# Expert stages: the gated half of the up products as three float32r products, and scatters without clears between them

## The reference

```python
h_NM2H = jnp.einsum('md,ndh->nmh', x_MD, Wl1) + bl1[:, None, :]
a_NMH, b_NMH = (h_NM2H[..., :H], h_NM2H[..., H:])
y_NMD = jnp.einsum('nmh,nhd->nmd', jax.nn.silu(a_NMH) * b_NMH, Wl2) + bl2[:, None, :]
ew_MN = ew_MN.at[jnp.arange(M)[:, None], idx_MK].set(val_MK)
y_MD = jnp.einsum('mn,nmd->md', ew_MN, y_NMD)
```

## Time and profile before

| | before |
|---|---|
| time, median of 3 runs | 1177.89 us (1176.38 to 1179.65) |
| the profiled execution, its own time | 1185.97 us |
| its span, first to last instruction | 1184.1 us |
| mean granted TensorE clock | 0.834 |
| PE busy | 842.3 us (71%) |
| POOL busy | 731.5 us (62%) |
| DVE busy | 705.8 us (60%) |
| ACT busy | 571.2 us (48%) |
| DMA moved | 142.69 MB, 121 GB/s |

### The profile page before, as it was taken

The page is one execution under the profiler, slowest core; times in us unless marked ns, Lnnn a source line. Parts: engine busy times, 40 slices in busy tenths (PEclk is TensorE's granted clock), DMA queues, the critical chain, the costliest instruction groups (busy, mean ns, idle before and its releaser), DMA issues.

```text
span 1184.1 us, 19270 instructions
## 1 busy us (share of the span) xinstructions
PE 842.3 (71%) x4480; PEld 667.6 (56%) x4481; DVE 705.8 (60%) x2510; ACT 571.2 (48%) x1588; POOL 731.5 (62%) x1127
## 2 busy tenths in 40 slices
PE   3787867767429889898755667566721988988981
PEld 1565656646318778787722334333420877877871
DVE  5697867845524444444647888889750343655555
ACT  3776646642213233333768887988620333323320
POOL 3017876736745777777710378787784576766774
PEclk9779878866659999999977888778755999999996
DMA  6022232112255555556412232231233555777874
GB/s 182 19 59 86 89 87 76 53 36 70 79 129 166 148 155 155 157 155 196 129 54 71 85 98 80 76 95 45 60 104 79 153 153 179 230 216 227 241 211 138
DMA packets 160255, 142.69 MB, mean 121 GB/s; under 512 B 17817, under 2 KB 133154, under 8 KB 160070
## 3 DMA queue, kind: packets, MB, share of 16 engines
q1 hardware_dynamic: 121744, 70.98, 21.9%
q10 hardware_dynamic: 20854, 37.24, 10.3%
q0 software_dynamic: 17600, 33.87, 8.4%
HBM read 93.47 MB, written 50.37 MB: 121 GB/s over the span
## 4 chain that ended last, share of the span: by engine, by line
PE 43%; ACT 17%; DVE 11%; issue 11%; POOL 7%; another core or an unknown queue 6%; DMA 2%; ACTq 2%; DVEq 1%; SPq 0%; POOLq 0%
PE banks L1055 16%; PE banks L1075 6%; POOL queue_dram L567 5%; PE banks L927 4%; PE banks L953 4%; ACT qkv L737 2%; ACT hmix L636 2%; PE banks L960 2%; PE banks L1110 2%; ACT gated L746 2%; PE banks L1063 2%; PE banks L1111 2%; PE banks L981 1%; DVE gated L1403 1%
## 5 line engine op out<-in xcount | busy, mean ns | idle before, releaser
L580 POOL DMA_INDIRECT result_dram<-ytile,result_row x284 | 277.9, 979 | 165.4 <-remote 57.5
L567 POOL DMA_INDIRECT queue_dram<-hffn,place_i x256 | 300.3, 1173 | 60.4 <-issue 46.0
L1055 PE MATMUL banks<-xt,tile_up 128*128 128x256 f32 x1136 | 286.2, 397 | 35.8 <-DVE gated L1403 31.6
L746 ACT ACTIVATE gated<-banks,tile_bias 128x256 f32<-128x256 f32 x284 | 119.2, 473 | 302.7 <-PE banks L1055 130.5
L1055 PEld LDWEIGHTS banks<-xt,tile_up 128*128 128x128 f32 x1136 | 213.4, 198 | 69.2 <-issue 28.3
L1403 DVE SCALAR_TENSOR_TENSOR gated<-banks,tile_bias,gated 128x256 f32<-128x256 f32 x284 | 124.2, 480 | 170.9 <-ACT gated L746 104.5
L1075 PE MATMUL banks<-wdown_sb,gated 128*128 x1136 | 156.4, 281 | 17.4 <-DVE ytile L1411 9.1
L1075 PEld LDWEIGHTS banks<-wdown_sb,gated 128*128 128x128 f32 x1136 | 142.0, 195 | 22.1 <-issue 21.7
L542 POOL MEMSET spacer<- 128x176 f32 x508 | 133.2, 262 | 0.4
L557 POOL COPY hffn<-top_f 128x4 f32<-128x4 f32 x32 | 5.0, 190 | 203.6 <-DVE place_i L1301 203.6
L1411 DVE TENSOR_TENSOR ytile<-banks,down_bias_sb 128x256 f32<-128x256 f32 x142 | 59.5, 419 | 76.1 <-remote 41.4
(11 more groups left out here) (203 smaller groups left out, 1570.2 us busy)
## 6 DMA issues: line engine op xcount, KB each, us to landing
tile_up<-w_up ACTq DMA_DIRECT2D x142, 256.0 KB
xtile<-queue_dram SPq DMA_DIRECT2D x142, 130.0 KB
qkv<-result_dram SPq DMA_DIRECT2D x24, 512.0 KB
x_dram<-xres SPq DMA_DIRECT2D x32, 256.0 KB
result_dram<-ytile,result_row POOLq DMA_INDIRECT x284
xin<-x SPq DMA_DIRECT2D x16, 256.0 KB
xold<-x SPq DMA_DIRECT2D x16, 256.0 KB
queue_dram<-hffn,place_i POOLq DMA_INDIRECT x256
```

What stands on the lines that cost most here:

```text
L567: nc.gpsimd.indirect_dma_start(queue_dram, bass.IndirectOffsetOnAxis(ap=place_i[s][:, at:at + 1], axis=0), hffn[s][c][:, j, :], None).then ...
L580: nc.gpsimd.indirect_dma_start(result_dram, bass.IndirectOffsetOnAxis(ap=result_row[i % SLOTS][:, h:h + 1], axis=0), ytile[i % SLOTS][:, h ...
L746: last = nc.scalar.activation(gated[i % GSLOTS][:, h, :], ps_up[i % 2][:, h, :], ACT.Silu, bias=tile_bias[i % STEP][:, h:h + 1])
L1055: last = nc.tensor.matmul(ps_up[i % 2][:, h, :], tile_up[i % WSLOTS][:, h * P:(h + 1) * P], xt[i % 2][:], start=True, stop=True)
```

## The change

On PE, `up` keeps the two float32 matmuls of the silu half, on `xt`. Each of the two matmuls of the gated half becomes three float32r matmuls into the same accumulator: head of the weights by head of x, head of the weights by rest of x, rest of the weights by head of x. The heads are the values as a float32r write rounds them, the rests are what is left; the product of the two rests is left out.

- The weights are split once, on GpSimd, before its first scatter: three DMAs of 1 MB each in a chain through an SBUF buffer, a copy and a subtraction of [128, 2048], and two DMAs of 1 MB out. The expert stages then load 384 KB a tile from `up_dram` and not 256 KB from the input.
- x is split a tile: `empty_x` on ACT gets a second copy ahead of the old one, and DVE gets `rest_of_x(i+4)`, a subtraction of 128x256 behind `add_bias(i)`. PE waits for it (`rest_ready`) before the first float32r matmul.
- In the expert stages the scatters have no clear between them. In the scatters of routed rows the clears stay; one semaphore wait (`numbered`) goes.
- Three startup semaphores become one.

```diff
@@ POOL
-                    last = nc.gpsimd.tensor_copy(hffn[s][c][:, :, D], k_sb[:, bass.ds(at + (K_TOKEN + c * TPC), TPC)])
-                last.then_inc(numbered, 1)
+                    nc.gpsimd.tensor_copy(hffn[s][c][:, :, D], k_sb[:, bass.ds(at + (K_TOKEN + c * TPC), TPC)])
...
-                pool.wait_ge(numbered, m)
-                pool.sem_inc(place_taken, 1)
...
                             ytile[i % SLOTS][:, h, :], None, bounds_check=NO_RESULT - 1, oob_is_err=False).then_inc(y_stored[i % SLOTS], 16)
-                        space(i * XPARTS + h, count * XPARTS)
...
+            ups = w_up.rearrange("p (e a n) -> p e a n", a=2, n=HID)
+            head, rest = up_parts
+            plain = rest[:].bitcast(F32)
+            pool.dma_start(plain, ups[:, :, 0, :]).then_inc(up_moved, 16)
+            pool.wait_ge(up_moved, 16)
+            pool.dma_start(up_dram[:, :, 0, :], plain).then_inc(up_moved, 16)
+            pool.wait_ge(up_moved, 2 * 16)
+            pool.dma_start(plain, ups[:, :, 1, :]).then_inc(up_moved, 16)
+            pool.wait_ge(up_moved, 3 * 16)
+            nc.gpsimd.tensor_copy(head[:], plain).then_inc(up_split, 1)
+            pool.wait_ge(up_split, 1)
+            nc.gpsimd.tensor_tensor(rest[:], plain, head[:].bitcast(F32), ALU.subtract).then_inc(up_split, 1)
+            pool.wait_ge(up_split, 2)
+            for i, part in enumerate(up_parts):
+                pool.dma_start(up_dram[:, :, 1 + i, :], part[:].bitcast(F32)).then_inc(up_moved, 16)
@@ ACT
                     act.wait_ge(xtile_turned, done(f, t))
+                    nc.scalar.activation(x_parts[i % 2][:, 0, :], ps_xt[i % 2], ACT.Copy)
                     nc.scalar.activation(xt[i % 2][:], ps_xt[i % 2], ACT.Copy).then_inc(xt_ready, 1)
...
-                    nc.scalar.dma_start(tile_up[i % WSLOTS][:], w_up[:, bass.ds(e * (2 * HID), 2 * HID)]).then_inc(tile_up_in[i % WSLOTS], 16)
+                    nc.scalar.dma_start(tile_up[i % WSLOTS][:], up_dram[:, bass.ds(e, 1), :, :].rearrange("p e k n -> p (e k) n")).then_inc(tile_up_in[i % WSLOTS], 16)
...
+                act.wait_ge(up_moved, 5 * 16)
@@ PE
-                    for h in range(2 * HCH):
-                        last = nc.tensor.matmul(ps_up[i % 2][:, h, :], tile_up[i % WSLOTS][:, h * P:(h + 1) * P], xt[i % 2][:],
-                                                start=True, stop=True)
+                    for h in range(HCH):
+                        nc.tensor.matmul(ps_up[i % 2][:, h, :], tile_up[i % WSLOTS][:, 0, h * P:(h + 1) * P], xt[i % 2][:],
+                                         start=True, stop=True)
+                    pe.wait_ge(rest_ready, done(f, t))
+                    for h in range(HCH):
+                        head, rest = (tile_up[i % WSLOTS][:, 1 + part, h * P:(h + 1) * P].bitcast(F32R) for part in range(2))
+                        dst = ps_up[i % 2][:, HCH + h, :]
+                        nc.tensor.matmul(dst, head, x_parts[i % 2][:, 0, :], start=True, stop=False)
+                        nc.tensor.matmul(dst, head, x_parts[i % 2][:, 1, :], start=False, stop=False)
+                        last = nc.tensor.matmul(dst, rest, x_parts[i % 2][:, 0, :], start=False, stop=True)
                     last.then_inc(up_ready, 1)
@@ DVE
+                def rest_of_x(n, i):
+
+                    dve.wait_ge(xt_ready, done(f, n * STEP + i))
+                    nc.vector.tensor_tensor(x_parts[i % 2][:, 1, :], ps_xt[i % 2], x_parts[i % 2][:, 0, :].bitcast(F32),
+                                            ALU.subtract).then_inc(rest_ready, 1)
...
                         add_bias(n, i, e[i])
+                        if i + 4 < left:
+                            rest_of_x(n, i + 4)
```

28 lines of the change are left out of this document (18 added, 10 removed).

## The result

The changed kernel takes **1230.04 us** (median of 4 runs, 1223.46 to 1234.93) against 1178.1 us of the kernel before in the same measurement: a ratio of 1.0438, 95% interval 1.0379 to 1.0496. The forecast was 1152 us, and 1230 is beyond the range and on the other side. The profiled execution has a span of 1231.5 us, 47.4 more than before.

What follows compares the result with a forecast made beforehand. POOL's back-to-back scatters, holding back matmul ends until POOL pauses, were taken to set the pace. -27 + 1 = -26 us on 1185.97 gives 1160, carried to the median 1152 us; range 1132 to 1184.

Steps and rivals of the forecast that it cites:

- the pause as it is: POOL, expert stages: the pause after a run of scatters stays 1.97 us, so the cycle falls from 10.2 to 9.3 us.
- the third tile's end: PE's down products: the end that still comes through in time to make POOL's run six scatters; held, the run has four.
- rival 2: POOL's scatters: runs shrink to four or let no ends through without clears; -3 us, or +15 with longer pause; chance 0.12.
- The clears: POOL, expert stages: without clears a run of six takes 7.32 us, not 8.22; -42.6 us if every cycle keeps three tiles.
- The products: PE's `up`: a float32r matmul takes 0.11 us, the tile 2.64 instead of 2.84; counts nothing by itself.
- Rival 4: PE's `up`: a float32r matmul takes as long as a float32 record, 3.56 us a tile, +23 us, 1201 us; chance 0.10.
- The new wait: PE waiting for DVE's rest of x: one cycle in two shrinks to four scatters, 3.21 us a tile, -27 us.
- DVE, ACT, DMA: Expert stages: none becomes the bound; +1 us for stage ends, DMA 0, up to +6 us; DMA shares 0.70 and 0.86.
- The start: POOL's weight split: copy and subtraction 3.0 to 15 us each, ready between 45 and 70 us, before 84.33; cost 0.
- a sign of being wrong: Attention: the prediction is wrong if it gets longer by more than 5 us.
- rival 3: PE is the bound and the lateness its own, not POOL's; clears worth nothing, -28 us, 1150 us; chance 0.10.
- the late ends vanish: Expert stages: the prediction is wrong if matmul ends no longer reach the other engines late.

Runs made afterwards that it cites:

- e15: Kernel before without clears, each expert-stage scatter replaced by a GpSimd memset, experts' outputs left out, chip 2: 1123.0 us against 1186.3.
- e14: Kernel before with expert-stage clears of 352 columns instead of 176, chip 2: 1150.0 us against 1186.3, ratio 0.965.
- e1: Kernel before without clears in the expert stages, chip 15: 1075.1 us against 1080.2, ratio 0.994.
- e10: Kernel before without clears in the expert stages, chip 8: 1216.8 us against 1184.3, ratio 1.037.
- e6: Kernel before without clears in the expert stages, chip 9: 1075.2 us against 1080.0, ratio 0.995.
- e11: Changed kernel with the expert-stage clears put back, chip 8: 1195.9 us against 1184.3 for the kernel before, ratio 1.018.
- e13: Kernel before plus only x's split (ACT's second copy, `rest_of_x`) and PE's new wait, chip 2: 1188.1 us against 1186.3, ratio 1.006.
- e8: The whole change, unaltered, chip 9: 1063.2 us against 1080.0 for the kernel before, ratio 0.984.
- e7: Changed kernel with the expert-stage clears put back, chip 9: 1079.4 us against 1080.0 for the kernel before, ratio 1.000.
- e9: Kernel before with expert-stage clears of 352 columns instead of 176, chip 9: 1107.8 us against 1080.0, ratio 1.026.

## Why the prediction was wrong

**What bounds the kernel.** Right for the chip of that profile, and the best part of it: POOL's run and pause set the pace, and the scatters are what holds the ends. e15 shows it (2.83 us a tile and no late end without indirect DMAs), and e14 by a gain where POOL was slowed. The page TensorE: Matmul & The Clock Gate of the Trainium skill (The cost: per-tile semaphore tail) has a formula for the tail of completions; with one tile and one increment it gives an estimated 56 ns. The trace of e1 on chip 15 agrees with it to the order (0.10 us, the median from `up` to silu), and the trace of the kernel before does not (1.50 us).

**The failing step.** "I take the pause as it is, 1.97 us." The pause was held to be a constant and the run the thing to shorten. But with a gap of 0.42 us some ends are told while the run goes on, 51 of 91 late ones of `up`; with 0.30 us it is 14 of 96, and 33 of 105 in e10, where nothing but the clears had gone. So silu and gate went from beside the run into the pause ahead of `ytile`: 4.33 instead of 1.97 us. Of the 2.36 us more, silu and gate are 1.67 (407.58 to 409.25), and the other 0.69 is that the release itself comes 1.37 us after the run's end and not 0.68 (0.26 of it because a clear ended the run before). The cycle became 7.39 + 4.33 = 11.7 us, not 9.3. A second loss was not foreseen at all: 25 runs of a single tile for 10 before, 4.49 us each. An estimate from the means of both traces: 60 tiles in runs of six at 0.46 us more are 28 us, 15 more single tiles at 1.14 us are 17, together about the 44.9. Runs of four, which the prediction had at 3.38 us a tile, take 3.26 and cost nothing. The text had the seed of it twice: the third tile's end that "still comes through in time" within a run, and rival 2, by which scatters without the clears "let nothing through". Rival 2 was the mechanism, but it was priced as if only `ytile` stood in the pause (0.26 us more, +15 us), where 2.36 us more came.

**The clears.** Runs of six of 7.39 us (7.32 forecast), 1.28 a scatter (1.27): right. Their removal as a gain of -27 to -42.6 us: wrong in sign here, +32.5 us by the medians (e10, 25 to 64 by the ratio's interval), and -5 us on chips 15 and 9 (e1, e6).

**The products.** 0.12 us a float32r matmul (0.11), a tile of 2.70 us (2.64): right within 0.06, which is six times 0.01. Rival 4 falls.

**The new wait.** Its mechanism was seen: 12 runs of four in e11 for 4 before, and a cost of 0.6% alone (e13, interval 0.05 to 1.2%). In the changed kernel there are 23, near the one in two that was forecast, but also the 25 of two. It was netted into a gain; with the clears in place nothing was there to be netted against.

**DVE, ACT, DMA.** No bound anywhere: of DVE's new work PE waited 4.0 us in the whole changed kernel. The loads' queue went from the earlier trace rows 10.3% to 15.0%; the share of the stages, forecast at 0.70 and 0.86, stayed at 0.60 and 0.67, since they took longer. Even e8, at a tile of 2.71 us, has PE busy 119.50 of 120 us. Right.

**The start.** In time: 2.35 and 5.38 us for copy and subtraction, where the bounds were 3.0 and 15 each, so the copy lies below its lower one, and ready at 46.7. But 2.5 to 5 us were lost in attention on chip 9 (e7 and e8 against e6 and e9), and nobody waits for POOL then. That DVE paid for POOL's two operations, which the text gave up to 5 us and then put at 0, would explain it; no run takes the split alone. The result's first scatter comes 5.7 us later, past the 5 us that were named as a sign of being wrong, but on the chips with late ends this says little: the same attention has its first scatter of experts anywhere from 346.7 us (e10) to 363.1 (e13).

**The rivals and the range.** That PE leads if ends are told at once was weighed as rival 3, with 1150 us; on chips 15 and 9 it is the case, the late ends vanish, which the text had named as what would make it wrong, and there the change does gain, 17 us. Its other half, that the lateness is PE's own, falls with e15. The range was built as if one profile showed a property of the kernel. It shows the kernel on a chip, and the term that decided, how many ends come through a gap of 0.3 us, was on no row.
